# Expert-mixture stages of a hybrid kernel: a new order of the first block, and routing weights spread from one SBUF partition each instead of from a DRAM scratch

## What is computed

```
xt = layernorm(x)
shared = relu(xt @ sW1 + sb1) @ sW2 + sb2
probs = softmax(xt @ router_W + router_b)          # 15 experts
top_p, top_i = top_k(probs, 3)
cw = zeros((n, 15)); cw[token, top_i] = top_p       # the routing weights
h = relu(einsum('nd,edh->neh', xt, eW1) + eb1)
ye = einsum('neh,ehd->ned', h, eW2) + eb2
x = x + shared + einsum('ned,ne->nd', ye, cw)
```

## Time and profile before

| | |
|---|---|
| runs of the kernel, median (3 runs, 2230.51 to 2232.52 us) | 2231.68 us |
| the profiled execution's own time | 2236.0 us |
| its span | 2234.3 us |
| mean granted TensorE clock over the span | 0.926 |
| PE matmul busy | 1862.4 us (83%) |
| DVE busy | 1685.1 us (75%) |
| ACT busy | 1203.0 us (54%) |
| POOL busy | 914.2 us (41%) |

### The profile page before, as it was taken

The page is one execution under the profiler, slowest core; times in us unless marked ns, Lnnn a source line. Parts: engine busy times, 40 slices in busy tenths (PEclk is TensorE's granted clock), DMA queues, the critical chain, the costliest instruction groups (busy, mean ns, idle before and its releaser), DMA issues. The chain is left out here.

```text
span 2234.3 us, 31060 instructions
## 1 busy us (share of the span) xinstructions
PE 1862.4 (83%) x9650; PEld 1280.5 (57%) x9650; DVE 1685.1 (75%) x4185; ACT 1203.0 (54%) x2004; POOL 914.2 (41%) x887
## 2 busy tenths in 40 slices
PE   6886499998699967673499978999999999967998
PEld 4554377776577723332377755555555555536777
DVE  6997688876588879998588867766767767636886
ACT  3442266652466634442366654666665655545666
POOL 1110355542355522220355544534543544234555
PEclk8998699999799998876699989999999999978999
DMA  3000344420444410000244410000000000004444
GB/s 99 6 5 4 110 158 143 143 72 1 143 143 143 143 39 1 1 0 0 72 146 160 156 39 1 1 1 1 1 1 1 1 1 1 1 1 143 162 167 138
DMA packets 87704, 142.28 MB, mean 64 GB/s; under 512 B 12369, under 2 KB 24337, under 8 KB 87026
## 3 DMA queue, kind: packets, MB, share of 16 engines
q1 hardware_dynamic: 85232, 139.50, 18.7%
q10 hardware_dynamic: 2306, 0.78, 0.2%
HBM read 136.38 MB, written 3.87 MB: 63 GB/s over the span
## 5 line engine op out<-in xcount | busy, mean ns | idle before, releaser
L2336 ACT ACTIVATE soft_prob<-psum 128x1024 f32<-128x1024 f32 (+3 forms) x384 | 302.4, 812 | 203.9 <-PE psum L2216 202.2
L2428 DVE TENSOR_REDUCE soft_mx<-psum 128x1 f32<-128x512 f32 (+2 forms) x352 | 230.8, 687 | 116.4 <-PE psum L2286 79.5
L2286 PE MATMUL psum<-soft_own,soft_stack 128*128 128x512 f32 (+3 forms) x768 | 249.4, 377 | 24.4 <-DVE soft_mx L2424 10.5
L2216 PE MATMUL psum<-soft_stack,soft_own 128*128 128x512 f32 (+3 forms) x768 | 225.5, 377 | 2.8 <-POOL soft_stack L2193 2.2
L2424 DVE CUSTOM_DVE_ANT_0 psum<-psum,s_soft_sel 128x384 f32<-128x384 f32 (+1 forms) x256 | 157.2, 638 | 65.0 <-PE psum L2286 64.4
L2216 PEld LDWEIGHTS psum<-soft_stack,soft_own 128*128 128x128 f32 x768 | 125.2, 189 | 133.1 <-issue 80.8
L2286 PEld LDWEIGHTS psum<-soft_own,soft_stack 128*128 128x128 f32 x768 | 139.8, 193 | 92.6 <-DVE soft_mx L2428 43.0
L2199 POOL TENSOR_SCALAR_AFFINE_SELECT soft_prob<-soft_prob 128x256 f32<-128x256 f32 x256 | 102.5, 407 | 203.9 <-ACT soft_prob L2336 201.0
L163 POOL TENSOR_TENSOR norm_rstd<-norm_mv,s_const_minus_half 128x4 f32<-128x4 f32 x64 | 65.1, 1018 | 279.3 <-DVE norm_mv L158 273.2
L2233 PE MATMUL psum<-soft_prob,soft_v_pad 128*32 128x512 f32 (+3 forms) x1536 | 163.7, 498 | 3.5 <-ACT soft_prob L2336 2.1
L940 POOL TENSOR_TENSOR ffn1b_low<-ffn1b_full,ffn1b_high 128x512 fp32r<-128x512 f32 x80 | 103.0, 1293 | 105.0 <-ACT ffn1b_high L1083 82.5
(11 more groups left out here) (440 smaller groups left out, 4977.7 us busy)
## 6 DMA issues: line engine op xcount, KB each, us to landing
ffn0a_cwb<-ffn0a_cw_dram SPq DMA_DIRECT2D x120, 256.0 KB, 6.2
ffn0b_cwb<-ffn0b_cw_dram SPq DMA_DIRECT2D x120, 256.0 KB, 6.4
ffn1a_cwb<-ffn1a_cw_dram SPq DMA_DIRECT2D x120, 256.0 KB, 6.3
ffn1b_cwb<-ffn1b_cw_dram SPq DMA_DIRECT2D x120, 256.0 KB, 6.1
s_ffn_w<-in_ffn_w SPq DMA_DIRECT2D x4, 1024.0 KB, 8.0
out_x<-x SPq DMA_DIRECT2D x8, 256.0 KB, 7.4
x<-in_x SPq DMA_DIRECT2D x4, 384.0 KB, 7.5
mamba_coef_dram<-mamba_out_coef SPq DMA_DIRECT2D x8, 96.0 KB, 1.6
```

What stands on the lines that cost most here:

```text
L2216: ins = pe.matmul(e_ps[:, n % 2, j, low(n):BLK], own[:, u % 3, 2 * pair + j, kt * P:(kt + 1) * P], stack[:, u % HT, qb * BLK + low(n):(qb ...
L2286: ins = pe.matmul(per_head[:, n, :], stack[:, u % HT, i * P:(i + 1) * P], own[:, u % 3, g, half * BLK:half * BLK + width], start=(n == 0), ...
L2336: nc.scalar.activation(prob[:, done % PROBS, :, low(n):BLK], e_ps[:, n % 2, :, low(n):BLK], ACT.Exp, scale=float(HD) ** -0.5).then_inc(exp ...
L2428: nc.vector.tensor_reduce(mx[:, i, half, heads.start:heads.stop], bank[:, 0:width * len(heads)].rearrange("p (g k) -> p g k", k=width), AX ...
```

## The change

It has three parts, in every call of `ffn_stage` (the second only where the weights are split).

1. The spread. The DRAM scratch, its store and the semaphore `stored` go. Each of the 15 loads of a block reads its row straight from its partition of `cwx`, 128 times, and writes the 128 partitions as before. `copy_cwt` writes cwx ahead of cwt. Since the loads now read cwx itself, ACT waits before it overwrites cwx until all 15 loads of the block before have landed.
2. The weights' low parts. POOL makes only the first piece before it waits for the first block's `cw_parts`, then the second piece of w1, then the norm's reciprocal root for block 1, then two pieces of w2. The third pieces (experts 8 to 15) of both move to DVE, behind `scale(1)`.
3. The order on PE and ACT in the first block. `transpose_cw(0)` stands directly behind up(3), and tokens(1) and route(1) behind it; ACT copies block 1's tokens before the first expert's parts. PE no longer waits for DVE's memsets before the first routing.

```diff
@@ spread, on SP
-                if q >= 2:
-                    sp.wait_ge(scaled_ready, E * (q - 1))
-                sp.dma_start(cw_dram[q % 2, :, :], cwx[EXACT:EXACT + E, :]).then_inc(stored, 16)
-                sp.wait_ge(stored, 16 * (q + 1))
                 for j in range(E // PIECE):
                     k = E // PIECE * q + j
                     if k >= PIECES_KEPT:
                         sp.wait_ge(scaled_ready, PIECE * (k - PIECES_KEPT + 1))
-                    src = cw_dram[q % 2, PIECE * j:PIECE * (j + 1), :].rearrange("e t -> (e t)").unsqueeze(0)
-                    sp.dma_start(cwb[:, k % PIECES_KEPT, :, :].rearrange("p e t -> p (e t)"),
-                                 src.to_broadcast([P, PIECE * BLK])).then_inc(piece_loaded[k % PIECES_KEPT], 16)
+                    sp.dma_start(cwb[:, k % PIECES_KEPT, 0, :], cwx[EXACT + j:EXACT + j + 1, :].unsqueeze(1).to_broadcast([1, P, BLK]))\
+                        .then_inc(piece_loaded[k % PIECES_KEPT], 16)
@@ POOL
             if split:
-                for which, i in ((0, 0), (0, 1), (1, 0), (0, 2), (1, 1), (1, 2)):
-                    low_weights(which, i)
+                low_weights(0, 0)
+                pool.wait_ge(cw_ready, 1)
+                low_weights(0, 1)
             norm.invert(pool, 1)
+            if split:
+                low_weights(1, 0)
+                low_weights(1, 1)
@@ PE, route(q)
                 if q:
-                    pe.wait_ge(cwx_ready, q)
+                    pe.wait_ge(cwt_ready, q)
@@ PE, order (up and down wait for w1_low_rest and w2_low_rest at expert 8)
-            pe.wait_ge(cw_one, 1)
             route(0)
             for n in range(EXPERTS):
                 g, e = divmod(n, NE)
                 up(n)
                 if n == H_BANKS - 1:
                     transpose_cw(0)
+                    tokens(1)
+                    route(1)
                 if n >= LAG:
                     down(n - LAG)
-                if e == 0 and g + 1 < more_blocks:
+                if e == 0 and 0 < g and g + 1 < more_blocks:
                     tokens(g + 1)
-                if e == 3 and g + 1 < BLOCKS:
+                if e == 3 and 0 < g and g + 1 < BLOCKS:
                     route(g + 1)
@@ ACT, copy_cwt(q)
-                nc.scalar.copy(cwt[:, q % 2, :], cwt_ps[0:B2_ROWS, :, :]).then_inc(cwt_ready, 1)
                 if q:
-                    act.wait_ge(stored, 16 * q)
+                    for j in range(E):
+                        k = E * (q - 1) + j
+                        act.wait_ge(piece_loaded[k % PIECES_KEPT], 16 * (k // PIECES_KEPT + 1))
                 nc.scalar.copy(cwx[EXACT:EXACT + NE, :], cwt_ps[EXACT:EXACT + NE, :, :]).then_inc(cwx_ready, 1)
+                nc.scalar.copy(cwt[:, q % 2, :], cwt_ps[0:B2_ROWS, :, :]).then_inc(cwt_ready, 1)
@@ ACT, order
             copy_cwt(0)
+            copy_x(1)
             for n in range(EXPERTS):
                 g, e = divmod(n, NE)
                 parts_of(n)
-                if e == 1 and g + 1 < more_blocks:
+                if e == 1 and 0 < g and g + 1 < more_blocks:
                     copy_x(g + 1)
@@ DVE, ahead of the first expert
             norm.scale(dve, 1)
+            if split:
+                dve.wait_ge(w_high, 3)
+                low_weights(w1_parts, w["w1"], w1_low_rest)
+                low_weights(w2_parts, w["w2"], w2_low_rest)
```

More of the change, by code:

```diff
@@ L866, in ffn_stage @@
         top8 = sb("top8", [P, GT, 8])
-        cw_dram = nc.dram_tensor(f"{name}_cw_dram", [2, E, BLK], F32, kind="Internal").ap()
         logit_ready, shifted, exp_done = sem("logit_ready"), sem("shifted"), sem("exp_done")
@@ L875, in ffn_stage @@
         logit_used, cw_link, b2_high, b2_ready = sem("logit_used"), sem("cw_link"), sem("b2_high"), sem("b2_ready")
-        xt_high, xt_split, stored = sem("xt_high"), sem("xt_split"), sem("stored")
+        xt_high, xt_split = sem("xt_high"), sem("xt_split")
         piece_loaded = [sem(f"piece_loaded{i}") for i in range(PIECES_KEPT)]
         W_PIECES = (0, 4, 8, NE)
+        w1_low_rest, w2_low_rest = sem("w1_low_rest"), sem("w2_low_rest")
         more_blocks = BLOCKS + (out is None)
@@ L930, in low_weights @@
                 some = slice(W_PIECES[i], W_PIECES[i + 1])
-                pool.wait_ge(w_high, 1 if which == 0 and i == 0 else 2 if which == 0 else 3)
+                pool.wait_ge(w_high, (1 if i == 0 else 2) if which == 0 else 3)
                 dst, src, done = ((w1_parts, w["w1"], w1_ready), (w2_parts, w["w2"], w2_ready))[which]
@@ L985, in up @@
                         pe.wait_ge(scaled_ready, routed_up_to(m))
-                if split and g == 0 and e in W_PIECES:
+                if split and g == 0 and e in W_PIECES[:2]:
                     pe.wait_ge(w1_ready, W_PIECES.index(e) + 1)
+                if split and g == 0 and e == W_PIECES[2]:
+                    pe.wait_ge(w1_low_rest, 1)
                 if e == 0:
@@ L1005, in down @@
                     pe.matmul(y_ps[:, g % 2, :], b2_parts[:, :], cwt[:, g % 2, :], start=True, stop=False)
-                if split and g == 0 and e in W_PIECES:
+                if split and g == 0 and e in W_PIECES[:2]:
                     pe.wait_ge(w2_ready, W_PIECES.index(e) + 1)
+                if split and g == 0 and e == W_PIECES[2]:
+                    pe.wait_ge(w2_low_rest, 1)
                 pe.wait_ge(high_ready, n + 1)
@@ L1088, in copy_cwt @@
                     act.wait_ge(down_done, NE * (q - 2) + 1)
+                if q:
+                    for j in range(E):
+                        k = E * (q - 1) + j
+                        act.wait_ge(piece_loaded[k % PIECES_KEPT], 16 * (k // PIECES_KEPT + 1))
+                nc.scalar.copy(cwx[EXACT:EXACT + NE, :], cwt_ps[EXACT:EXACT + NE, :, :]).then_inc(cwx_ready, 1)
                 nc.scalar.copy(cwt[:, q % 2, :], cwt_ps[0:B2_ROWS, :, :]).then_inc(cwt_ready, 1)
-                if q:
-                    act.wait_ge(stored, 16 * q)
-                nc.scalar.copy(cwx[EXACT:EXACT + NE, :], cwt_ps[EXACT:EXACT + NE, :, :]).then_inc(cwx_ready, 1)
             def copy_y(g):
@@ L1197, in add, with low_weights @@
                 nc.vector.tensor_tensor(xg, back_ps[:, :, :], xg, ALU.add).then_inc(x_added, 1)
+            def low_weights(dst, src, done):
+                some = slice(W_PIECES[2], NE)
+                nc.vector.tensor_tensor(dst[1][:, some, :], src[:, some, :], dst[0][:, some, :], ALU.subtract)\
+                    .then_inc(done, 1)
             norm.resume(dve)
```

## The result

The changed kernel takes **5600.1 us** (median of 4 runs, 5598.6 to 5603.1) against 2231.4 us before (also of 4 runs): a ratio of 2.510 (95% interval 2.506 to 2.514). The forecast was slower, 6175 us, with 5900 to 6750 as the range of its own mechanism. The wide range, from 2165 us, holds it.

A forecast was written before the change was run, and what follows sets the result against it. PE was taken to bound mid-mixture, a chain to the first load each start. 2236.0 + 3999.6 for slow loads - 56 for the start = 6180, less 4.3: about 6175 us; range 2165 to 6750.

The forecast's parts named there:

- its own mechanism: In every block's loads from cwx, one stream at a time from one partition: 5900 to 6750 us, chance 0.55.
- rival A: Loads from cwx as fast as before and hidden, only the new start counts: 2178 us, up to 2182; chance 0.32.
- rival B: Loads from cwx: one partition gives several streams, or different partitions' loads run side by side: 3811 or 2628 us; chance 0.12.
- What bounds the kernel, and the start's chain: PE bounds mid-mixture; at the start, first loads leave 15.9 (ffn1a, ffn1b), 14.7 (ffn0a), 9.7 us (ffn0b) earlier: -56 us.
- DVE's added low parts: First block: two more subtractions on DVE, 3 to 4.8 us in all; 1.2 to 3 us show in ffn1a and ffn1b.
- One partition serves one stream: Each load's source partition serves one engine's stream at a time: 26.6 GB/s, so 9.85 us a load.
- loads of a block in a row without overlap: In each block 15 loads follow one another, 147.8 us; a stage's stretch goes from 209.0 to 1208.9 us.
- the 16 stand before the same partition together: Engines take their shares of the loads in order of issue, so loads of different partitions don't run beside each other.
- ACT's wait and the single cwx: Between blocks ACT waits for all loads before overwriting cwx; then 0.58 us of copy and 2.8 to the first bytes.
- The rate in a mixture: In the profile after, the DMA rate in a mixture falls from 152 to about 26 GB/s.
- The granted clock: In the mixtures the clock would be half for most of the time, 0.50 as at ffn0a's start, and cost nothing.
- a load was to land up to 148 us after its issue: In the profile after, a block's last load lands up to 148 us after issue, as loads queue; 6 us before.

The follow-up runs named there:

- read_128_parts: The changed kernel with every load reading 2 KB from each of the 128 partitions of x, not one partition of cwx 128 times (wrong weights): 2173 us.
- rows_apart: The changed kernel with right weights, but expert rows laid out so that no two successive loads read the same group of four partitions: 3883.1 us, ratio 1.738.
- low_parts_only: The kernel with the new order and DRAM scratch, but PE's and ACT's first-block order put back, so only the low parts move: 2218.4 us, ratio 0.992.

## Why the prediction was right, point by point

The direction, the mechanism and the order of size were right: one partition of SBUF gives no more than one engine's stream, and this makes the kernel 2.5 times as long. The range held the time only because it had to reach down to rival A; the range of the forecast's own mechanism, 5900 to 6750 us, missed it. One step failed, the argument against the second half of rival B: it is the fourth point.

- **What bounds the kernel, and the start's chain.** Right. The forecast for hidden loads (rival A) was 2178 us, 54 below the kernel before. The new order with the scratch measured 2177.7 and 2180.1, but that this agrees so closely is luck: rival A has no store, and those runs have one, beside a kernel before of 2234.7 and 2234.5. The run nearest to rival A is read_128_parts, 63 us below the kernel before beside it. The first load was put at +10.1 in ffn1a and at +11.9 in ffn0a. In the kernel after they are at 2765.89 - 2755.73 = +10.2 (SP's queue and ACT's first cast in ffn1a) and +11.7. In ffn0b it is at +7.5, from 18.8, 11.3 us gained where 9.7 were forecast; in ffn1b at +8.8, from 26.6, 17.9 where 15.9 were. All four starts bring the first load 60 us forward, not 56.
- **DVE's added low parts.** 3 to 4.8 us were set, and they take 2.35. But the norm's scaling ahead of them takes 3.01 us, not 1.11, since POOL's weight pieces now run beside it. Sum 5.4, against 4.1 to 5.9.
- **One partition serves one stream.** This step decided the forecast. Its reason, that no row had more than 3.3 GB/s for one partition, could only say that more had not been seen. It was put as 26.6 GB/s and 9.85 us a load, from the best stretch of the trace; the loads have 27.2 and 9.63. That part of the error is 4 x 8 x 15 x 0.22 = 106 us. The limit belongs to four neighbouring partitions together, and 16 engines share it; the prediction spoke of one partition alone.
- **The term that was mis-sized: loads of a block in a row without overlap.** I argued against rival B that "the 16 stand before the same partition together". Across a change of group they don't: a block takes 14.5 us less than its loads in a row. Over 32 blocks that is 464 us, and the rates at the changes (up to 59 GB/s) and rows_apart show the mechanism. In ffn0a the stretch from first load to last product (254.27 to 1318.7, by the row below) is 1064 us, not 1208.9. Four times the difference is 578, and 6175 - 578 = 5597.

```profile
L1189 DVE SCALAR_TENSOR_TENSOR ffn0a_scaled<-psum,s_ffn_b,ffn0a_cwb x120: 736/751/752, 266.5 to 1318.7; 128x512 f32<-128x512 f32 x120
```

- **ACT's wait and the single cwx.** Right in kind: between two blocks' loads lie the copy and 2.3 us (2.8 were set), and everything else of a block is in the loads' shadow.
- **What the profile would show.** The rate in a mixture (30, not 26 GB/s) follows from the two points above. The granted clock came out as foreseen, 0.50 in most of ffn0a's first block and 0.62 from 300 to 1300 us. One sign was wrong: a load was to land up to 148 us after its issue. The longest takes 32 us. SP's queue takes a new load only as an old one is done, as its own durations say (min/median/max in ns):

```profile
L895 SPq DMA_DIRECT2D ffn0a_cwb<-ffn0a_cwx x120: 469/9583/9878, 254.3 to 1295.2; - x120
```

With a landing of 30.5 and a pitch of 9.63 about three loads are in flight. The wait is then seen at SP's issue of a load, and not between issue and landing.

## What to carry to other kernels

Ask of a load not only how many bytes it moves and onto how many partitions, but from how many it reads: a row spread over 128 partitions is read 128 times, and from SBUF all of these come out of one place, at 27.2 GB/s here. A scratch in DRAM, with a store of 1.6 us that is hidden in all blocks but the first, was the cheap way. And judge a bundle by its parts: here a change worth 2.5% lay under one that costs more than 150%.

## What the runs showed that was not expected

- One partition of SBUF gives the DMA engines 27.2 GB/s, four neighbours (96 to 99) no more together (25), and four that lie four apart 102; the same 2 KB row read 128 times from DRAM comes at 380 GB/s.
- Loads issued in order on one queue overlap by nearly 5 us for each change of group, on average: 79.2 us a block with 14 changes, 132.9 with 3.
- A load whose source has 4 partitions ran on 4 engines (5760 packets fewer in 480 loads), though its target has 128: 10.7 us on one group, 2.6 on four.
- DVE's small operations are held by POOL's passes over the weights far beyond their own length: 0.69 us of work took 6.84 before and 0.69 again in low_parts_only, which moves those passes, and four scalings of 1.11 take 3.01 in the kernel after.
